# Attention scores on TensorE: mask products ahead of the score products

## The reference, cut to what matters

```python
q = q / jnp.sqrt(jnp.asarray(D, dtype=q.dtype))
attention = jnp.einsum('bhtd,bhkd->bhtk', q, k)
mask = jnp.where(qpos - kpos >= 0, 0.0, NEG_INF).astype(attention.dtype)
attention = attention + mask[None, None]
activation = jax.nn.softmax(attention, axis=-1)
x = jnp.einsum('bhtk,bhkd->bhtd', activation, v)
```

## Time and profile before

| what | us |
|---|---|
| median of 3 timed runs | 485.72 |
| lowest, highest of them | 483.19, 486.51 |
| span of the profiled execution | 485.8 |
| TensorE busy in it | 439.9 (91%) |
| VectorE, ScalarE, GpSimd busy | 359.8, 312.8, 302.7 |

### The profile page before, as it was taken

One profiled execution on the slowest core, in us unless ns is written; L12 is line 12 of the kernel. 1 busy time (PEld: TensorE's weight loads), 2 busy tenths in 40 slices (PEclk: granted clock), 3 DMA queues, 4 the chain that ended last, 5 costly groups with the idle time before them and its releaser, 6 DMA issues.

```text
span 485.8 us, 12527 instructions
## 1 busy us (share of the span) xinstructions
PE 439.9 (91%) x3983; PEld 329.3 (68%) x3987; DVE 359.8 (74%) x804; ACT 312.8 (64%) x709; POOL 302.7 (62%) x439
## 2 busy tenths in 40 slices
PE   8888897988998989999889999998999899979995
PEld 4666565665666666666555688786877788868884
DVE  6885997987878877778774387585765777566987
ACT  2756676775867677767677676565565766555552
POOL 1326887997887888887888500755547487845300
PEclk9999999998999999999999999999999999989998
DMA  8776798999875555666356337787777767821762
GB/s 233 229 240 233 230 329 294 295 332 331 266 232 153 156 164 174 173 177 168 119 165 255 90 84 214 242 290 225 225 234 247 239 195 258 299 60 35 245 204 65
DMA packets 60415, 102.00 MB, mean 210 GB/s; under 512 B 11045, under 2 KB 29226, under 8 KB 59328
## 3 DMA queue, kind: packets, MB, share of 16 engines
q1 hardware_dynamic: 55872, 92.74, 61.2%
q0 software_dynamic: 4480, 8.47, 5.2%
HBM read 62.49 MB, written 39.46 MB: 210 GB/s over the span
## 4 chain that ended last, share of the span: by engine, by line
PE 62%; ACT 7%; POOL 6%; issue 5%; DVE 4%; SPq 4%; DMA 2%; another core or an unknown queue 2%; DVEq 0%; ACTq 0%; POOLq 0%
PE ps L850 11%; PE ps L848 11%; PE ps L849 11%; PE ps L917 6%; PE ps L978 6%; PE ps L925 4%; ACT sb_work L706 4%; POOL sb_work L620 3%; POOL xs L596 2%; PE ps L998 2%; DMA sb_ring<-qk 2%; PE ps L1143 2%; PE ps L981 2%; SPq L471 2%
## 5 line engine op out<-in xcount | busy, mean ns | idle before, releaser
L1343 DVE TENSOR_REDUCE sb_blockmax<-ps 128x6 f32<-128x768 f32 x128 | 121.5, 956 | 37.2 <-PE ps L925 32.4
L706 ACT ACTIVATE sb_work<-ps 128x768 f32<-128x768 f32 x128 | 104.7, 818 | 64.7 <-PE ps L913 63.5
L648 POOL DMA_INDIRECT ys<-sb_v_all,sb_xn_all x76 | 81.3, 1069 | 72.3 <-DVE sb_v_all L1464 52.6
L620 POOL TENSOR_SCALAR_AFFINE_SELECT sb_work<-sb_work 128x512 f32<-128x512 f32 x128 | 82.2, 646 | 27.6 <-ACT sb_work L706 25.5
L849 PE MATMUL ps<-sb_ring,sb_wb 128*128 128x512 f32 (+1 forms) x231 | 83.6, 362 | 0.0
L1443 DVE TENSOR_TENSOR sb_v_all<-ps,sb_v_all 128x512 f32<-128x512 f32 (+1 forms) x93 | 57.5, 618 | 24.4 <-ACT sb_v_all L796 10.6
L596 POOL DMA_INDIRECT xs<-sb_xn_all,sb_posu x64 | 62.9, 983 | 10.6 <-issue 10.6
L917 PE MATMUL ps<-sb_ring 32*128 32x256 f32 x256 | 49.5, 377 | 20.7 <-ACT sb_work L706 10.1
L796 ACT ACTIVATE sb_v_all<-ps 128x512 f32<-128x512 f32 (+1 forms) x93 | 49.7, 534 | 10.5 <-PE ps L850 5.4
L917 PEld LDWEIGHTS ps<-sb_ring 32*128 32x128 f32 x256 | 25.6, 183 | 44.9 <-issue 38.4
L848 PE MATMUL ps<-sb_ring,sb_wb 128*128 128x512 f32 (+1 forms) x138 | 51.6, 374 | 3.3 <-issue 1.8
(11 more groups left out here) (168 smaller groups left out, 1089.0 us busy)
## 6 DMA issues: line engine op xcount, KB each, us to landing
sb_wb<-wd SPq DMA_DIRECT2D x75, 384.0 KB
sb_ring<-qk SPq DMA_DIRECT2D x64, 256.0 KB
wd<-sb_wb SPq DMA_DIRECT2D x8, 1152.0 KB, 5.9
xs<-sb_o_all SPq DMA_DIRECT2D x19, 260.0 KB, 4.2
qk<-sb_ring SPq DMA_DIRECT2D x32, 128.0 KB
sb_work<-ys SPq DMA_DIRECT2D x16, 256.0 KB, 3.2
sb_xn_all<-xs SPq DMA_DIRECT2D x15, 260.0 KB
sb_o_all<-w SPq DMA_DIRECT2D x8, 384.0 KB, 3.9
```

What stands on the lines that cost most here:

```text
L620: pool.affine_select(out=o, in_=o, compare_op=ALU.is_ge, fill=0.0, base=0, pattern=[[0, 4], [1, 128]], channel_multiplier=-1)\
L648: pool.indirect_dma_start(out=ys_d, out_offset=bass.IndirectOffsetOnAxis(ap=row, axis=0), in_=yst[i % NYS][:, EMB * j:EMB * j + EMB], in_o ...
L706: act.activation(part.rearrange("p (k h q) -> p h k q", h=2, q=128), ps[:, 4:6, 0:HEAD].rearrange("p h (k q) -> p h k q", q=128), ACT.Exp, ...
L1343: dve.tensor_reduce(blockmax[:, a:b + 1, 0:3], ps[:, a:b + 1, 0:HEAD].rearrange("p h (k c) -> p h k c", c=128), AX.X, ALU.max).then_inc(s[ ...
```

## The change

The mask product of a head now starts the accumulation of its bank (start=True), ahead of the score products, which all add to it; `s0` closes it. The two mask products stand in front of the wait for the loaded queries and keys, and of the waits for q4b and for the exponential, but behind the wait for the reduction of S. The semaphore S is raised by the last `s0`, which now lies ahead of the last `t1`.

```diff
             def s1(m, h):
                 q, k = q4[m % NK][rows_of(h), 128:256], k4[m % NK][rows_of(h), :]
-                return pe.matmul(S[h][:, 0:256], q, k, start=True, stop=False, skip_group_check=True)
+                return pe.matmul(S[h][:, 0:256], q, k, start=False, stop=False, skip_group_check=True)
 
             def s0(m, h):
                 q, k = q4[m % NK][rows_of(h), 0:128], k4[m % NK][rows_of(h), 0:128]
-                return pe.matmul(S[h][:, 256:HEAD], q, k, start=False, stop=False, skip_group_check=True)
-
-            def masked(h):
+                return pe.matmul(S[h][:, 256:HEAD], q, k, start=False, stop=True, skip_group_check=True)
+
+            def mask(h):
                 out = S[h][:, 128:HEAD].rearrange("p (k c) -> p k c", k=2)
                 return pe.matmul(out, ident_b[:, :], mask_b[:, :].unsqueeze(1).to_broadcast([128, 2, 128]),
-                                 start=False, stop=True, skip_group_check=True)
+                                 start=True, stop=False, skip_group_check=True)
 
             def scores(n, half):
...
                 if isq(m):
-                    pe.wait_ge(s_qk[m % NK], m // NK * 16 + 16)
                     if m:
                         pe.wait_ge(s[("max0", "mx")[half]], m)
+                    mask(a)
+                    mask(b)
+                    pe.wait_ge(s_qk[m % NK], m // NK * 16 + 16)
                 if isq(n):
                     pe.wait_ge(s["q4b"], n + 1)
                     if n or half:
                         pe.wait_ge(s["ex"], 2 * n + half)
...
                 if isq(m):
                     s0(m, a)
-                    s0(m, b)
+                    s0(m, b).then_inc(s["S"], 1)
                 if isq(n):
                     t1(n, c)
                     t1(n, d).then_inc(s["ST"], 1)
-                if isq(m):
-                    masked(a)
-                    masked(b).then_inc(s["S"], 1)
```

## The result

| | median us | runs | lowest, highest |
|---|---|---|---|
| before | 485.72 | 7 | 483.14, 491.57 |
| after | 488.85 | 7 | 488.06, 490.84 |

The ratio is 1.0099, with a 95% interval of 1.0066 to 1.0132: slower by 3 to 6 us, where +5.8 was forecast. The profiled execution of the changed kernel has a span of 488.8 us. Its own time is 490.52, so 1.7 us lie around the span; the forecast counted from the span of before, which it took for the execution's time.

The account below looks back on a forecast made before the run. The bound was taken to be a loop: first block, TensorE's work up to the second block, exponential, next first block. 0.8 + 1.6 + 5.1 - 1.7 = +5.8 us on 485.8 gives 491.6 us, range 489 to 496.

Parts of the forecast that it names:

- The last sign named: Attention, 132 to 257 us: the forecast is wrong if the step is not longer than 3.47 us on average.
- L998 0.37 after the block: TensorE's transposes start 0.37 us after the first block once the masks behind it are gone, instead of 0.61.
- The price of the masks: Ahead of the second block: two masks after the sums make it start 0.32 us later; low bound 0.23.
- free step: Attention step whose sums do not wait for another engine: loses 0.32 - 0.18 = 0.14 us.
- waiting ones: Attention steps whose sums wait for GpSimd, ScalarE or VectorE: nothing saved behind the first block, each loses 0.32 us.
- the 1.7 it took off for GpSimd and VectorE: Attention: a slower loop meets GpSimd's backlog less and VectorE's earlier reduction shortens 5.0 us of waits; together -1.7 us.
- The late exponential: 132 to 257 us: the second block's exponential already starts late, 0.17 us on average, hiding 3.9 us of 9.0.
- Rival C: Attention: nothing absorbs the cost, all 58 steps pay, +14.6 us to 500.4 us; chance 8%.
- Up to 132 us: Attention: 0.8 us kept of 4.0 from 51 to 110 us, where loads bound; 1.6 us from 110 to 132.
- The experts' stage: After the attention: starts later by the same amount, +5.8 us, and is otherwise as before.
- A (the exchange is even): Masks after the sums cost 0.23 rather than 0.32 us; 486 to 488 us, say 487.0; chance 30%.
- B (faster, through VectorE): Attention: the reduction starts 0.32 us sooner, so transposes and sums come sooner; 480.8 us; chance 8%.

Follow-up runs that it names:

- 6: Changed kernel with the second half's two mask products issued twice: 498.87 us, ratio 1.0292 to the kernel before.
- 7: Changed kernel with the first half's two mask products issued twice: 490.58 us, ratio 1.0136 to the kernel before.
- experiment 5: Changed kernel, but from step 2 on the second half's masks stand between the transposes and the sums: 492.51 us, ratio 1.0187 to the kernel before.
- experiments 9 to 11: GpSimd's indirect DMAs moved to steps 45 to 62, in the kernel before (523.84 and 521.22 us) and in the changed kernel (528.48 us).
- chip B: Both kernels run once more without edits on another chip: before 465.93 us, after 474.43 us, ratio 1.0137.
- experiment 3: Masks ahead of the score products in the first half only, second half as in the kernel before: 466.73 us, ratio 0.9983 to the kernel before.
- 12: Masks ahead only in the first half of every fourth step, all else as in the kernel before: 485.31 us, ratio 1.0017.
- 9: Kernel before with GpSimd's 64 indirect DMAs spread over steps 45 to 62 instead of 23 to 62: 523.84 us.
- experiments 9 and 11: Kernel before with GpSimd's indirect DMAs spread over steps 45 to 62, run on two chips: 523.84 and 521.22 us.

## Why the prediction was right, and where its sizes were off

**Direction and mechanism held.** From step 24 on the first block stands 0.14 to 0.17 us behind the exponential in both kernels, the second behind the sums. The last sign named, a step over 3.47 us, came (3.532); "L998 0.37 after the block" came only in one step of four (0.38; otherwise 0.51 or 0.62). Doubling the masks in either place (6, 7) shows which place counts.

**The price of the masks was right to 0.01 us where products alone set it.** Forecast: mask 0.33 us after L981, block 0.32 after the mask, 1.85 us between the blocks in a free step. Measured: 0.34, 0.32 and 1.86. That the three rows of other places could be put together like this was the useful part of the reading: what a product costs at its start depends on the tiling before it and on its own, here hardly on its type. (The prediction puts every change at some 0.2 us; from row tiles to the full array the trace has 0.15.) The rule that the Trainium skill gives (TensorEngine Tiling (Array Packing), Key Properties: a change of tiling mode drains the TensorE) is borne out in direction by experiment 5, where an order with one change fewer gains 0.11 us per free step.

**Free steps were counted too cheaply, waiting ones too dearly.** A free step was to get 0.18 us back behind the first block. In every fourth step (44 above) the transposes then met ScalarE's copy L736, and started only 0.10 sooner. With neither late signals nor GpSimd's backlog (experiments 9 to 11, steps 24 to 44), the distance between the blocks rises by 0.15 us in one kind of step in four and by 0.21 in the other three; no kind costs the 0.32 of a waiting step. In the first pair, over all 36 steps, it rose by 0.19 us on average, 7.0 us together; the forecast's terms for this are 9.0, less the 1.7 it took off for GpSimd and VectorE, so 7.3. That these agree is in part luck, since the two prices err in opposite ways. The reason given for VectorE's share of the 1.7 holds in its direction: the transposes that wait for it start 0.02 to 0.3 us sooner after the block.

**The late exponential hid more than forecast**: 36 x 0.14 = 5.1 us instead of 3.9. So the stretch lost 2.2 us instead of 5.1 less its part of the 1.7. It depends on the chip: on chip B, without the delay, the same stretch lost 5.6 us and the ratio is 1.0137. Rival C (nothing absorbs) asks for more than that, 9.0 us in this stretch; on chip B the blocks moved apart by only 0.12 us on average, to 2.04 us as in the first pair, but from 1.92 and not from 1.84.

**Up to 132 us** the forecast kept 2.4 us, and here it was furthest off: the first pair shows -1.5, chip B +0.3. The reason given, that waits for loads swallow the cost, fits only in part. Of the -1.5 us 1.4 is there when step 2 begins, after the kernel before has had TensorE at 1.2 GHz for 3.4 us. The six steps from 18 to 24 took 21.61 us before and 21.88 after, but before with 3.4 us at 1.2 GHz. Runs with the second half's masks in the old place and no such stretch took 20.07 (experiment 3), 20.10 (12) and 20.90 (9). Against 21.88, and 21.31 on chip B, that is 1.0 to 1.8 us for the changed order, where 1.6 was forecast. As far as runs of other chips can stand beside it, this term came out near its size, and the clock hid it, a term that the forecast does not have. The idle time before L917 for loads fell from 10.1 to 1.6 us in the first pair, and from 6.5 to 0.2 on chip B. That masks in the wait keep the clock up is a possible reason; it was not tried.

**The experts' stage** was to be unchanged. In the first pair's profiles it took 2.3 us more, through 10.2 instead of 3.4 us at 1.2 GHz; in the pair of chip B it was equal. The long stretch is not bound to the change: experiments 5 to 7, with the changed order or a version of it, have 6.8 us or less at 1.2 GHz before the last few us of this stage and take 215.7 to 215.8 us for it, while the kernel before in experiment 9 has 10.2 us in two pieces and takes 219.1. Nor was it in all seven timed executions: 10.2 us at half the clock alone would bring the mean over 486 us down to 0.99, and those at 0.999 and 1.000 still took 488.10 and 488.06 us. How the 3.1 us between the medians divides stays open.

**What of the number is luck.** Forecast +5.8; the medians differ by 3.1, the spans by 3.0. The 3.0 is made of -1.5, +2.2 and +2.3 us, of which the forecast had the sign of one. The first and the last go with stretches at 1.2 GHz, and they happened to cancel in part. The estimates at a full clock bear the forecast's sum out better than the medians do: 5.3 us, and on chip B 8.3, where the 3.9 that the late exponential was to hide have to be added to the 5.8.

**Rivals.** A (the exchange is even) falls by the start distances and by experiments 9 to 11; the 0.7 us that the attention lost in the first pair's profiles would by itself have suited it. B (faster, through VectorE) falls by the time: the reduction did start right after s0 and the transposes a little sooner, but the second block is later all the same. C falls with the 14.6 us that it asks for.

## What to carry to other kernels

Where an engine's queue is a ring of work with one wait in it, moving work behind or ahead of a block is a rotation: what counts is on which side of the wait the work comes to stand, and whether a wait that used to be hidden beside it is now bare. Count the changes of array tiling in the new order and price them from start-to-start distances at other places of the same trace. Work moved into an idle gap gains nothing once the engine's own work fills the gap (experiment 3), and a cost that is hidden by a delay of one chip comes out on another. Look at where the granted clock falls in both profiles before a difference in a stage is put down to the change.

## What the runs showed that had not been expected

In the first pair and on chips C and D signals from TensorE come late while GpSimd issues indirect DMAs: in most steps from 23 on the signal of the sums came 0.6 to 0.9 us after the start of their last product, in both kernels, and 0.32 us before step 23 and, on chip B, nearly always. In the kernel before, the exponential that waits for the second block, whose signal follows, started 0.22 us after its products on average and 0.8 at most, while the signal of the mask products behind them was on time. In the changed kernel the block comes later, and the exponential starts 0.08 us after it. Without the DMAs it is on time (experiments 9 and 11). On chip B, with the DMAs, none of this is seen, and the experts' stage, which issues such DMAs too, takes 201.2 us against 215 to 219. That the late signals explain that difference was not tried.
